# Cross attention, self attention and a ternary feed-forward on one core: 180 waits in a branch not taken, another DVE order in the self stage, gathers and buffers at the stage ends

## The chip, the cores and the metric

One core of one Trainium2 chip runs the whole program. The time is that of the device for one execution, in microseconds (us). The engines are called as in the profile: PE (TensorE), DVE (VectorE), ACT (ScalarE), POOL (GpSimd), SP (SyncE, which here issues the DMAs).

## The reference

x is 64 batches of 64 tokens by 512, the context 64 batches of 512 keys by 512. All is fp32; 16 heads of 32.

```python
x = x + cross_attention(layernorm(x), ctx, ctx, mask)      # mask: True keys get -inf
x = x + self_attention(layernorm(x))   # scores * mask of the 64 largest of 64: a plain softmax
x = x + ffn(layernorm(x))              # relu(x @ Wq1.T + b1) @ Wq2.T + b2, 512 -> 2048 -> 512

def _quantize(W):                      # the two weights of the feed-forward
    gamma = jnp.mean(jnp.abs(W))
    return jnp.clip(jnp.round(W / (gamma + EPS)), -1.0, 1.0)
```

The mask of batch 0 holds for all. It leaves keys of the last of four tiles of 128 alone, so the kernel takes the branch that works on that tile only.

## The kernel before, in words

Products are made in pairs of fp32r values: each operand is split into a high part (a copy to fp32r) and a low part (the rest, by a subtraction on DVE), and `split_products` (L340 to L350) issues three matmuls for each chunk of 128. The feed-forward's weights are -1, 0 or 1, so there only the moving side is split.

There are three stages, each with its own program on each engine, in order: cross attention in 16 units of 256 tokens, self attention in 16 units of 256, feed-forward in 8 units of 512. `run_steps` writes out units 0 and 1, puts two units into the body of a hardware loop, and writes out the last two ("last_but_one", "last"). So the self loop's body is two units and runs six times, with five jumps back; the feed-forward loop's runs twice. `choose` reads a flag and runs the cross program for the last key tile (the If branch) or the one for all tiles (the Else branch), which stands behind it in each engine's instructions; the self and feed-forward programs come after both.

The order of the work is written out by hand, engine by engine, and semaphores carry the dependences. Two PSUM banks `project_0/1` take all projections in turn (class `Banks`); a product waits until its bank's last contents were copied out.

One self unit on PE (`self_pe`, step at L1460): scores of token tile 0, the output product O1 of the unit before (o_proj waits on the low half of the attended values, `self_at_lo`), queries of the next unit Q0, Q1, scores of tile 1, transposes of tile 0's probabilities, keys K0, attention product of tile 0, K1, values V0, transposes 1, V1, attention product 1, O0. On DVE (`self_dve`, step at L1665): maxima(0) (a reduction L1611 and a subtraction L1613), residual of O1 (L1630), statistics of the unit after next, divide(0) (L1619, L415, L419), normalise (L464, which waits for the POOL's reciprocal root L1177), block transpose (L427), maxima(1), the high and low half of the attended values (L1590, L1594), divide(1), keys_out (L546), values_out twice (L552), the low part of the next x (`self_x_lo`, L531), then in the loop two ternary quantisations of feed-forward weights (L1232, L1235), residual of O0, the low half for tile 1. `self_ln_gather` lets SP issue four DMAs (L435) that bring the transposed blocks into place; ACT then makes the high part of x (L527, after V1 is done) and DVE the low part.

At the end of cross attention the units' last steps already prepare the self stage: `self_ln_normalise` and `self_ln_transpose` for self units 0 (S_FIRST) and 1 (S_SECOND), whose gathers SP issues (L631, L641), the second one after the store of cross token tile 0. At the end of the self stage `last_step` on DVE (L1634) prepares feed-forward unit 0 (F_FIRST): `ff_x_norm` is one buffer of two token tiles, so tiles 2 and 3 are normalised after the low part of tiles 0 and 1 is made. In feed-forward the same steps stand between the splits of the hidden values (L1822 to L1829).

## Time and profile before

| | us |
|---|---|
| median of 3 runs | 1780.06 (1777.68 to 1786.38) |
| profiled execution | 1779.26 |
| its span, first to last instruction | 1777.4 |
| granted PE clock, mean | 0.982 |
| PE busy / DVE busy / ACT busy / POOL busy | 1678.3 / 1068.4 / 697.7 / 215.0 |

```profile
PE   6899999999999999969989889899789999999999
PEclk9899999999999999989999999999999999999999
PE 83%; DVE 7%; issue 4%; ACT 3%; DMA 2%; POOL 1%; SPq 0%; DVEq 0%; POOLq 0%; ACTq 0%
q8 instruction: 145, 2.38, 0.6%
```

The first two lines cut the span into 40 slices of 44 us and give the busy share of PE and the clock granted to it in tenths (9 is 90% or more). The third splits the chain of work that ended last by engine; "issue" is time in which nothing that the profile shows was waited for. The fourth is the DMA queue that brings instructions: packets, MB, share of the DMA engines. Cross attention runs to about 790 us, self attention to about 1313, feed-forward to the end.

### The profile page before, as it was taken

To read this page: it belongs to the slowest core of one execution; us is meant where nothing else is said; L and a number is where in the kernel's file an instruction comes from. 1 tells how busy PE (TensorE), PEld (TensorE's weight loads), DVE (VectorE), ACT (ScalarE), POOL (GpSimd) and SP (SyncE) were. 2 spreads that over 40 slices of the span, in tenths; PEclk is the share of its full clock that TensorE was granted. 3 is DMA by queue.
4 is the path that set the end of the run, shared out by engine and by line. 5 is a ranking of instruction groups with operands and counts; after the bars stand their busy time and mean duration, and the time that the engine had idled before them with its cause. 6 is when DMAs were issued, how large, how long until landed. Compare 5 with 4: busy or idle time off the path is not lost.

```text
span 1777.4 us, 38416 instructions
## 1 busy us (share of the span) xinstructions
PE 1678.3 (94%) x16012; PEld 1401.2 (79%) x16012; DVE 1068.4 (60%) x1492; ACT 697.7 (39%) x1657; POOL 215.0 (12%) x300
## 2 busy tenths in 40 slices
PE   6899999999999999969989889899789999999999
PEld 4788888888888888858878778788678888888887
DVE  3655555555555555757767767767766555556543
ACT  2555555555555555647222222222222222222221
POOL 1000000000000000112121121121130222012200
PEclk9899999999999999989999999999999999999999
DMA  6011111111111112433111111211212121112110
GB/s 214 13 60 60 61 61 60 61 60 61 60 61 60 60 53 72 172 116 104 61 38 49 61 38 49 61 38 49 81 58 62 34 71 60 60 24 71 36 36 24
DMA packets 83529, 112.52 MB, mean 63 GB/s; under 512 B 7840, under 2 KB 48928, under 8 KB 82080
## 3 DMA queue, kind: packets, MB, share of 16 engines
q1 hardware_dynamic: 83360, 109.95, 19.6%
q8 instruction: 145, 2.38, 0.6%
q14 instruction: 24, 0.20, 0.0%
HBM read 67.97 MB, written 25.17 MB: 52 GB/s over the span
## 4 chain that ended last, share of the span: by engine, by line
PE 83%; DVE 7%; issue 4%; ACT 3%; DMA 2%; POOL 1%; SPq 0%; DVEq 0%; POOLq 0%; ACTq 0%
PE project L347 45%; PE project L1282 13%; PE scores L715 4%; PE scores L1775 3%; PE scores L1773 3%; PE probs_t_psum L1775 3%; PE probs_t_psum L1773 3%; PE probs_t_psum L724 3%; PE attended_t L741 2%; PE probs_t_psum L1391 1%; PE scores L519 1%; PE attended_t L1410 1%; DMA x<-self_residual 1%; DVE self_residual L1630 1%; DVE self_scores_shifted L1613 1%
## 5 line engine op out<-in xcount | busy, mean ns | idle before, releaser
L1282 PE MATMUL project<-ff_xt,w_ternary 128*128 128x512 f32 x1024 | 253.1, 389 | 0.0
L1282 PEld LDWEIGHTS project<-ff_xt,w_ternary 128*128 128x128 f32 x1024 | 192.2, 188 | 40.1 <-issue 0.2
L1292 ACT ACTIVATE hidden<-project,b_sb 128x512 f32<-128x512 f32 x128 | 88.2, 689 | 339.8 <-PE project L1282 339.8
L901 ACT ACTIVATE cross_scores_probs<-cross_scores_probs,exp_bias,logit_scale 128x128 f32<-128x128 f32 x256 | 122.7, 482 | 101.9 <-DVE exp_bias L1044 101.9
L347 PE MATMUL project<-self_xt_hi,self_w_hi 128*128 128x256 f32 x512 | 149.5, 292 | 7.0 <-DVE self_xt_lo L531 6.0
L347 PE MATMUL project<-self_xt_lo,self_w_hi 128*128 128x256 f32 x512 | 145.9, 285 | 0.0
L347 PE MATMUL project<-self_xt_hi,self_w_lo 128*128 128x256 f32 x512 | 145.7, 285 | 0.0
L901 ACT ACTIVATE cross_probs<-cross_scores,exp_bias,logit_scale 128x128 f32<-128x128 f32 x256 | 122.8, 483 | 1.6 <-DVE exp_bias L1044 1.6
L347 PE MATMUL project<-ctx_hi,cross_w_hi 128*128 128x512 f32 x256 | 106.5, 416 | 15.2 <-DVE ctx_lo L1063 15.2
L347 PE MATMUL project<-cross_w_hi,ctx_hi 128*128 128x512 f32 x256 | 108.7, 425 | 0.0
L347 PEld LDWEIGHTS project<-self_xt_hi,self_w_hi 128*128 128x128 f32 x512 | 99.3, 194 | 10.2 <-issue 6.9
L347 PE MATMUL project<-ctx_hi,cross_w_lo 128*128 128x512 f32 x256 | 101.4, 396 | 0.0
L347 PE MATMUL project<-ctx_lo,cross_w_hi 128*128 128x512 f32 x256 | 101.3, 396 | 0.0
L347 PE MATMUL project<-cross_w_hi,ctx_lo 128*128 128x512 f32 x256 | 100.6, 393 | 0.0
L347 PE MATMUL project<-cross_w_lo,ctx_hi 128*128 128x512 f32 x256 | 100.3, 392 | 0.0
L347 PEld LDWEIGHTS project<-self_xt_lo,self_w_hi 128*128 128x128 f32 x512 | 99.5, 194 | 0.6
L347 PEld LDWEIGHTS project<-self_xt_hi,self_w_lo 128*128 128x128 f32 x512 | 99.2, 194 | 0.0
L480 POOL TENSOR_TENSOR self_residual<-self_x,bo_sb 128x512 f32<-128x512 f32 x32 | 52.8, 1672 | 370.4 <-DMA x<-self_residual 370.4
L918 ACT ACTIVATE cross_probs_t<-probs_t_psum 128x1024 f32<-128x1024 f32 x64 | 65.3, 1021 | 81.2 <-PE probs_t_psum L724 81.2
L1297 DVE CAST hidden_hi_a<-hidden 128x512 fp32r<-128x512 f32 x64 | 29.0, 453 | 109.1 <-ACT hidden L1292 109.1
L1523 ACT ACTIVATE self_probs<-self_scores_shifted 128x1024 f32<-128x1024 f32 x32 | 33.9, 1060 | 152.8 <-DVE self_scores_shifted L1613 152.8
L1186 POOL TENSOR_TENSOR var_eps<-mean_var,ln_eps 128x2 f32<-128x2 f32 x16 | 5.1, 316 | 646.5 <-DVE mean_var L1008 646.5
(169 smaller groups left out, 4085.7 us busy)
## 6 DMA issues: line engine op xcount, KB each, us to landing
ctx_raw<-in_ctx SPq DMA_DIRECT2D x64, 256.0 KB, 3.9
cross_xt_raw<-in_x_t SPq DMA_DIRECT2D x64, 128.0 KB, 2.1
cross_x<-in_x SPq DMA_DIRECT2D x32, 256.0 KB, 2.9
x<-cross_x SPq DMA_DIRECT2D x32, 256.0 KB, 2.0
self_x<-x SPq DMA_DIRECT2D x32, 256.0 KB, 2.8
self_x_norm<-self_blocks_t SPq DMA_DIRECT2D x64, 128.0 KB, 2.9
ff_w_raw<-in_w SPq DMA_DIRECT2D x2, 4096.0 KB, 14.6
x<-self_residual SPq DMA_DIRECT2D x32, 256.0 KB, 2.0
```

The source lines that it names most:

```text
L347: last = nc.tensor.matmul(out_ap, a, b, start=(n == 0), stop=(n == 3 * len(pairs) - 1))
L480: e.tensor_tensor(sres[:, parity(v), t, :], sx[:, parity(v), t, :], bo_sb[:], ALU.add).then_inc(G.res, 1)
L715: last = nc.tensor.matmul(S[half:half + SEQ, slot * n:(slot + 1) * n], cq_t[rows, c, K.batch(q), :], keys, start=True, stop=True)
L724: last = nc.tensor.transpose(PT[:, i * P:i * P + P], c_p[q % 2][:, i * P:i * P + P], ident[:])
L741: last = nc.tensor.matmul(PV[rows, t, col:col + SEQ], cv[:, parity(u), q if K.kt == 1 else k, DK * head:DK * head + DK], c_pt[:, at:at + S ...
L901: last = nc.scalar.activation(c_p[buf][:, cols], c_s[buf][:, cols], ACT.Exp, bias=exp_bias[:, buf, g:g + 1], scale=logit_scale[:, parity(u ...
L918: nc.scalar.activation(c_pt[:], PT[:], ACT.Copy).then_inc(C.pt_ready, 1)
L1282: last = nc.tensor.matmul(PJ[m % 2][:], w1_q[:, c, cols], x_t[parity(v)][:, c].rearrange("p n a r -> p (n a r)"), start=(c == 0 and x_t is ...
L1292: nc.scalar.activation(h_raw[:, m % 2, :], PJ[m % 2][:], ACT.Relu, bias=b1_sb[:, m:m + 1]).then_inc(h_relu, 1)
L1523: nc.scalar.activation(s_p[:], s_d[:], ACT.Exp, scale=SCORE_SCALE) \
L1773: nc.tensor.matmul(YB[t], h_hi[m % 4][:, rows], w2_q[:, m, :], start=(m == 0), stop=False)
L1775: last = nc.tensor.matmul(YB[t], h_lo[m % 4][:, rows], w2_q[:, m, :], start=False, stop=(m == FC - 1))
```

## The change

Five edits. (1) In the Else branch of `choose`, which is not run here, PE gets 180 waits on a semaphore that has long been set. (2) In the self unit, DVE does maxima(1) before normalising, the block transpose after divide(1), and the two quantisations between the values' copies. (3) At the end of cross attention, DVE divides tile 2 and makes the low half of tile 0 before it normalises S_FIRST, and SP issues the gather of S_SECOND before the store of cross tile 0. (4) The feed-forward's normalised x gets a second buffer, `fxn_1`; at the end of the self stage tiles 2 and 3 are normalised one step earlier, and the residual and maxima(1) come before the transpose and the low part. (5) In the feed-forward units, the normalising of tiles 2 and 3 and the second transpose move to earlier places.

```diff
+            fxn_1 = sb(st, "ff_x_norm_1", [P, 2, D])
+            fxn = [fxn_0, fxn_1]
...
                     e.dma_start(w_raw[:, 0].rearrange("p k n -> p (k n)"), w1).then_inc(fw_in[0], 16)
+                    self_ln_gather(e, S_SECOND)
...
                     if kind == "last" and t == K.nt - 1:
 
-                        self_ln_gather(e, S_SECOND)
                         load_self_x(e, Unit(1, 0))
...
                 values_out(u, v, 1)
+                divide(u, 2)
+                if K.nt == 2:
+                    a_lo(u, 0)
                 if not ahead:
                     self_ln_normalise(e, S_FIRST)
                     self_ln_transpose(e, S_FIRST)
-                divide(u, 2)
-                if K.nt == 2:
-                    a_lo(u, 0)
                 values_out(u, v, 2)
...
-            wait(e, fxt_lo_ready, total(v, 2, t // 2))
-            nc.vector.tensor_scalar(fxn[:, t % 2, :], fx[:, parity(v), t, :],
+            wait(e, fxt_lo_ready, total(v, 2, t // 2 - 1))
+            nc.vector.tensor_scalar(fxn[t // 2][:, t % 2, :], fx[:, parity(v), t, :],
...
             def last_step(u):
                 maxima(u, 0)
-                ff_x_lo(e, F_FIRST, 0)
                 values_out(None, u, 0)
                 divide(u, 0)
-                for t in range(2, FT):
-                    ff_ln_normalise(e, F_FIRST, t)
-                ff_ln_transpose(e, F_FIRST, 1)
                 residual(later(u, -1), 1, "last_but_one")
                 maxima(u, 1)
+                ff_ln_transpose(e, F_FIRST, 1)
+                ff_x_lo(e, F_FIRST, 0)
                 values_out(None, u, 1)
...
                 divide(u, 0)
                 if kind == "full":
                     self_ln_aggregate(e)
+                maxima(u, 1)
+                if kind == "full":
                     self_ln_normalise(e, w)
-                    self_ln_transpose(e, w)
-                maxima(u, 1)
                 a_hi(u)
                 a_lo(u, 0)
                 divide(u, 1)
+                if kind == "full":
+                    self_ln_transpose(e, w)
                 keys_out(u, v, kind)
                 if kind == "full":
                     values_out(u, v, 0)
+                    if not isinstance(u.half, int):
+                        for n in range(2):
+
+                            ternary(e, n, number(u) - 2, lambda k: total(u, 2, k - 4))
                     values_out(u, v, 1)
                     self_x_lo(e, w)
-                    if not isinstance(u.half, int):
-                        for n in range(2):
-
-                            ternary(e, n, number(u) - 2, lambda k: total(u, 2, k - 4))
                 else:
...
                     ff_ln_transpose(e, F_FIRST, 0)
+                    for t in range(2, FT):
+                        ff_ln_normalise(e, F_FIRST, t)
...
-                        if m in (2, 3, 6, 7):
-                            ff_ln_normalise(e, v, (0, 1, 2, 3)[(2, 3, 6, 7).index(m)])
-                        if m in (3, 7):
-                            ff_ln_transpose(e, v, m // 4)
+                        if m in (2, 3, 4, 5):
+                            ff_ln_normalise(e, v, m - 2)
+                        if m in (3, 6):
+                            ff_ln_transpose(e, v, m // 3 - 1)
...
+        PE_FILLER = 180
+
+        def choose(e, program, filler=0):
...
                 program(e, ALL_TILES)
                 e.nop()
+                for _ in range(filler):
+                    e.wait_ge(flag_ready, 1)
...
-            choose(e, cross_pe)
+            choose(e, cross_pe, PE_FILLER)
```

## Rows read from the trace of the kernel before

**Rows 1.** Busy time by stage: us, PE, PEld, DVE, ACT, POOL, PEclk, DMA, GB/s.

```profile
850.00:1245.00 395.00, 361.80 (x5046) 317.62 (x5049) 278.78 (x372) 98.78 (x144) 61.43 (x72) 0.97 0.18 50
1313.00:1777.40 464.40, 460.50 (x2032) 381.11 (x2030) 251.81 (x413) 100.19 (x140) 70.45 (x88) 1.00 0.17 49
```

**Rows 2.** The same view, stretches of the self loop.

```profile
860.30:1224.74 364.44, 331.91 (x4577) 291.15 (x4576) 256.62 (x340) 90.55 (x132) 56.02 (x67) 0.96 0.18 50
890.97:928.02 37.05, 31.95 (x418) 27.79 (x417) 23.46 (x31) 8.22 (x12) 5.61 (x8) 0.91 0.17 45
928.02:958.70 30.68, 29.00 (x417) 25.63 (x416) 23.44 (x30) 8.23 (x12) 4.90 (x7) 1.00 0.19 53
```

**Rows 3.** Timeline of PE at a jump back: start, us, operation, [idle before, releaser].

```profile
912.62 0.61 PE L519 MATMUL scores<-self_k_t,self_q_t 32*64 32x64 f32 x25 [1.92 <-issue]
915.95 1.34 PE L519 MATMUL scores<-self_k_t,self_q_t 32*64 32x64 f32 x39 [2.71 <-issue]
```

**Rows 4.** Instruction queues in 912:979 (self), 1420:1537 and 1539:1655 (feed-forward).

```profile
q8 instruction: 9, 0.15, 1.0%
...
q8 instruction: 4, 0.07, 0.2%
...
q14 instruction: 1, 0.01, 0.0%
```

**Rows 5.** Timeline of PE at the start of a unit without a jump.

```profile
946.86 0.39 PE L347 MATMUL project<-self_w_hi,self_at_lo 128*128 128x512 f32 x1
...
950.02 0.47 PE L347 MATMUL project<-self_w_hi,self_at_hi 128*128 128x512 f32 x1 [1.68 <-DVE self_at_lo L1594]
```

**Rows 6.** Timeline of DVE there.

```profile
943.56 0.69 DVE L552 TENSOR_TENSOR self_v<-project,bv_sb 128x512 f32<-128x512 f32 x1 [2.92 <-PE project L347]
...
945.87 0.48 DVE L1232 TENSOR_SCALAR ff_weight_scratch<-ff_w_raw,thresholds 128x512 f32 x1
...
947.93 0.75 DVE L1235 SCALAR_TENSOR_TENSOR w_ternary<-ff_w_raw,thresholds,ff_weight_scratch 128x512 f32 x1
...
949.20 0.68 DVE L1594 TENSOR_TENSOR self_at_lo<-attended_t,self_at_hi 128x512 fp32r<-128x512 f32 x1
```

**Rows 7.** Timelines of DVE and PE at the end of unit 1, without quantisation.

```profile
848.85 0.69 DVE L1594 TENSOR_TENSOR self_at_lo<-attended_t,self_at_hi 128x512 fp32r<-128x512 f32 x1
...
849.69 0.38 PE L1491 MATMUL attended_t<-abs_total,ones 128*128 128x2 f32 x2 [1.51 <-DVE abs_total L1700]
```

**Rows 8.** Timeline of DVE in the middle of a unit.

```profile
962.29 1.25 DVE L427 STREAM_TRANSPOSE self_blocks_t<-self_x_norm 128x1024 f32<-128x1024 f32 x1
...
965.82 0.68 DVE L1590 CAST self_at_hi<-attended_t 128x512 fp32r<-128x512 f32 x1
...
968.67 1.23 DVE L419 TENSOR_TENSOR self_probs<-self_probs,row_scale 128x1024 f32<-128x1024 f32 x1
```

**Rows 9.** End of cross attention: PE timeline, page's DMA issues, chain.

```profile
721.50 0.74 PE L724 MATMUL probs_t_psum<-ident,cross_scores_probs 128*128 128x128 f32 x5 [1.97 <-DVE cross_scores_probs L419]
...
self_x_norm<-self_blocks_t SPq DMA_DIRECT2D x64, 128.0 KB, 2.9
ff_w_raw<-in_w SPq DMA_DIRECT2D x2, 4096.0 KB, 14.6
...
760.79 1.25 DVE self_blocks_t L427
...
773.33 0.62 SPq L435
...
775.35 3.67 DMA self_x_norm<-self_blocks_t
...
781.56 7.49 PE project L347 x36
```

**Rows 10.** End of the self stage: the chain.

```profile
1287.54 4.36 PE project L347 x12
```

**Rows 11.** The chain: 12 matmuls of 512 columns at full clock.

```profile
722.56 2.75 PE project L347 x12
```

More of the change, by code:

```diff
@@ L244, in build @@
             fres = sb(st, "ff_residual", [P, 2, 4, D])
-            fxn = sb(st, "ff_x_norm", [P, 2, D])
+            fxn_0 = sb(st, "ff_x_norm_0", [P, 2, D])
             f_ln_t = sb(st, "ff_blocks_t", [P, 2 * D])
@@ L254, in build @@
             b2_sb = sb(st, "b2_sb", [P, D])
+            sb(st, "ff_gap_2", [P, 8])
+            fxn_1 = sb(st, "ff_x_norm_1", [P, 2, D])
+            fxn = [fxn_0, fxn_1]
             h_hi = [t[:, i, :] for t in (h_hi_a, h_hi_b) for i in range(2)]
@@ L1260, in ff_ln_transpose @@
             wait(e, f_ln_in, total(v, 128, 64 * n))
-            ln_blocks(fxn[:], f_ln_t[:]).then_inc(f_ln_t_done, 1)
+            ln_blocks(fxn[n][:], f_ln_t[:]).then_inc(f_ln_t_done, 1)
         def ff_ln_gather(e, v, n):
             wait(e, f_ln_t_done, total(v, 2, n + 1))
-            ln_gather(e, fxn[:], f_ln_t, f_ln_in)
-        fx_chunks = fxn[:].rearrange("p t (a c r) -> p c (t a) r", a=4, r=32)
+            ln_gather(e, fxn[n][:], f_ln_t, f_ln_in)
+        fx_chunks = [xn[:].rearrange("p t (a c r) -> p c (t a) r", a=4, r=32) for xn in fxn]
         def ff_x_hi(e, v, n):
             wait(e, f_ln_in, total(v, 128, 64 * n + 64))
-            nc.scalar.activation(fxt_hi[parity(v)][:, :, n], fx_chunks, ACT.Copy).then_inc(fxt_hi_ready, 1)
+            nc.scalar.activation(fxt_hi[parity(v)][:, :, n], fx_chunks[n], ACT.Copy).then_inc(fxt_hi_ready, 1)
         def ff_x_lo(e, v, n):
             wait(e, fxt_hi_ready, total(v, 2, n + 1))
-            nc.vector.tensor_tensor(fxt_lo[parity(v)][:, :, n], fx_chunks,
+            nc.vector.tensor_tensor(fxt_lo[parity(v)][:, :, n], fx_chunks[n],
                                     fxt_hi[parity(v)][:, :, n].bitcast(F32), ALU.subtract).then_inc(fxt_lo_ready, 1)
@@ L1680, in step @@
                     values_out(u, v, 0)
-                    values_out(u, v, 1)
-                    self_x_lo(e, w)
                     if not isinstance(u.half, int):
@@ L1686, in step @@
                             ternary(e, n, number(u) - 2, lambda k: total(u, 2, k - 4))
+                    values_out(u, v, 1)
+                    self_x_lo(e, w)
                 else:
@@ L1860, in ff_pool @@
             run_steps(e, F_UNITS, step)
-        def choose(e, program):
+        PE_FILLER = 180
+        def choose(e, program, filler=0):
             e.wait_ge(flag_ready, 1)
```

## The prediction

> **What bounds the kernel now.** I read the page's shares first (TensorE busy 94%, on 83% of the last chain), then the busy time by stage. Feed-forward is full, 460 us of TensorE in 464; the self loop has 362 in 395 [rows 1]. There TensorE waits, and there the change works.
>
> Next, the self loop by half-iteration, from one second scores product to the next. Without the jump back it takes 30.68 us at full clock; with the jump up to 37.05 at 0.91 of it [rows 2]. The 364.44 us of the group's first row hold six plain and five jumping stretches, so the five jumps cost 364.44 - 11 x 30.68 = 27.0 us. The matmul timeline shows how: after the last output product TensorE idles 1.92 us, runs 25 score matmuls, idles 2.71 us, and then works slowly: the other 39 take 1.34 us [rows 3]. "Issue" is the releaser: no semaphore was late. Instruction traffic says what was: in one iteration nine blocks of 16 KB are fetched (0.15 MB) [rows 4].
>
> The body of that loop has, as compiled, 1,692 TensorE instructions: 832 matmuls with a weight load each and 28 others. The 25 matmuls are 50 instructions behind two others at its head, so a block of 256 ends 52 in and the loop begins at place 204 of a block. 204 + 1,692 = 1,896, which touches 8 blocks; the ninth fetch is the one ahead. The feed-forward loop (1,062 instructions, 5 blocks) is fetched in its first pass and not in its second: 4 blocks, then none [rows 4]. So TensorE's store keeps a loop of 5 blocks and one ahead, and loses one of 8 and one ahead; 7 and one ahead lies between. Of the sizes 6, 7 and 8 that this leaves I take 8, the power of two.
>
> The other wait is at every unit's start: TensorE ends the first scores and stands 1.68 us before the output product, released by the low half of the attended values on DVE [rows 5]. That ran at 949.20, behind two weight quantisations that end at 948.68 [rows 6].
>
> **The change, part by part.**
>
> *180 waits in the branch not taken.* They are never run; they move what stands behind. In the compiled program one semaphore instruction carries two such waits, so I count 90 instructions: the loop begins at 204 + 90 - 256 = 38, and 38 + 1,692 = 1,730 touches 7 blocks. 180 single ones would give 128 + 1,692 = 1,820, 8 blocks. For a jump into kept blocks the bounds are 0 (no idle over 0.25 us stands at the feed-forward jump) and today's whole excess. I take 0, the feed-forward's, since 7 and one ahead fit a store of 8: **-27.0 us**. Feed-forward stays at 5 blocks. The cross loop lies before the filler, unchanged.
>
> The Trainium skill has a rule against this part (Runtime: NRT & Kernel Launch, Instruction fetch mechanics): prefetch is sequential over a window of two pages, and a taken branch outside it stalls for a fetch. By it the feed-forward loop's second pass would have fetched; the trace shows that it did not. The same section gives the PE 2,048 instructions, 8 blocks, by which the -27.0 holds.
>
> *Quantisation ahead of the second values.* Two of them take 948.68 - 945.87 = 2.81 us. DVE idles 2.92 us before that copy [rows 6]: they fit, with 0.1 to spare. Then nothing but the residual precedes the low half. The unit without quantisation shows what is left: output product ended 849.69 - 1.51 = 848.18, low half ended 849.54, 1.36 later [rows 7]. From a product end at 947.25 that is 948.61, and TensorE starts 0.14 behind it (950.02 against 949.88) at 948.75 instead of 950.02: 1.27 us a unit. The loop runs 12 units. At five of their ends the wait is covered by the jump today, but my 30.68 included it: 12 x 1.27 = **-15.2 us**, between 0 and 12 x 1.68 = 20.2.
>
> *Second maxima before normalising; block transpose after the second division.* Today normalising waits for POOL's root, the transpose runs from 962.29 for 1.25 us [rows 8], and only then come the maxima. The exponentials come sooner, but TensorE does not wait for them in the loop: 0. The transpose's move is the price. The division still hangs on the attention product before it: cast at 964.6, 4.1 us to the division's end (as 965.82 to 969.90 now [rows 8]), so 968.7; the transpose ends at 969.9 instead of 963.5. The gather's four DMAs behind it on SP take from 4.9 us (three issues of 0.65 and the median landing of 2.9) to 5.69 (773.33 to 779.02, after 11 us of idle queue) [rows 9], landing at 974.8 to 975.6. ACT wants them at 974.5, so the high and low parts of x come up to 1.1 us late, the low part ending at 978.0; the residual behind it on DVE waits for the product that ends at 978.13. Cost 0, with 0.1 us to spare. The key copy behind the transpose keeps its time. SP's store behind the gather waits for that later product anyway.
>
> *End of cross attention.* The division now precedes the self normalisation and transpose, which held it; TensorE waited for it 1.97 us, until 721.50 [rows 9]. **-2.0**. What is pushed back, the third values copy to 722.9, is wanted at 723.8. On SP the second self gather moves ahead of the first store: blocks are ready at 762.04, issued only at 773.33 [rows 9]. The 4 MB weight load before it on the queue goes out some 16 us before and takes 14.6 [rows 9], so it has landed. So it lands near 768 instead of 779.02, and the next bound is ACT's last copy of probabilities, done at 774.85: x parts done 4.25 us sooner, **-4.3**. The 36 matmuls behind took 7.49 us [rows 9]; at full clock 12 of 512 columns take 2.75 [rows 11], and 24 of 256 columns as much, with a little at the seams 5.6. With 1.7 us idle instead of 6.0 I count the drop gone (1.97 drew none above): **-1.9**. The cross store that the gather now precedes waits for a later product (773.33) in any case.
>
> *End of the self stage.* The second normalised buffer lets tokens 2 and 3 be normalised early (+1.0 us before the first maxima), and the residual that frees the bank goes ahead of transpose and low part. Now: low part, values, division, normalising, transpose, residual, product at 1287.54 [rows 10]. After: maxima until 1277.45, exponentials 1278.55, division 1281.35, residual 1282.0, product 1282.05. Low part and transpose then fall between second maxima and second values; the chain to the last output product keeps 11.35 of its 11.51 us: **-5.6**, down to 0 if the low part binds again, up to 7.2 if the slow product (4.36 for 12 [rows 10], 2.75 at full clock [rows 11]) speeds up.
>
> *Feed-forward order and buffer.* TensorE has no idle there [rows 1]; cover is 464 us of its own work: 0.
>
> Sum: 27.0 + 15.2 + 2.0 + 4.3 + 1.9 + 5.6 = 56.0. The profiled execution took 1,779.26 us (span 1,777.4), 0.8 under the median of 1,780.06. 1,779.3 - 56.0 = 1,723.3; on the median 1,724.
>
> **Rivals.**
> *One fetch at each jump, whatever the blocks.* The first block then has 218 instructions, some 6.5 us of work, so the second stall goes and only the 1.6 to 1.9 us one stays: 5 x 1.6, net of the low-half wait it covers, +8: **1,732**. For: the first pass of every loop fetches. Against: feed-forward's second pass. The skill's two-page rule, above, is this case.
>
> *Still 8 blocks* (the filler counts 180, or the store keeps under 8). With 128 instructions in the first block both stalls stay. Left are 7 x 1.27 + 13.8 = 22.7: **1,757**. Against: the two waits to an instruction.
>
> *The order gives little.* 0.1 us to spare at two places; half of it and the self end lost, about 15 us: **1,739**.
>
> *Slower: the late gather.* DVE runs in order, so a gather later than about 975.7 delays x's low part, residual, low half and TensorE one for one, in 14 units. To eat 56 us it must be 4 us later in each, so take over 9.8 us where 4.9 to 5.7 are seen [rows 9]; at 10.5 it costs 14 x 4.7 = 66: **1,790**. The loop's lighter queue speaks against.
>
> **How the numbers follow.** Forecast 0.76 (own range 1,717 to 1,734: the upper bounds of two terms give 5.0 and 1.6 more, the clock's 1.9 and half the order's 7.6 may fail), one fetch 0.10, order 0.05, 8 blocks 0.07, slower 0.02. 1,717 to 1,740 takes in the first three and leaves out 0.09. A measurement of this kernel tells about 0.5% (9 us) from no change. Faster by more than that: the first four cases but for 0.02 in which a late gather eats most, 0.96; the same 0.02; slower 0.02.
>
> **What would show it.** Instruction fetches in a loop pass after the first: 0, not 9. Every half-iteration near 29.4 us at clock 1.00; no issue wait in the scores. The wait on the low half near 0.4 us. The self gather issued near 760 and landed by 768; the product at 1287.54 some 5.5 us sooner relative to the loop's end. Wrong would be: nine fetches still, DVE waiting on the high part of x past the output product, or a new TensorE wait on the values' bank.

## The result and the profile after

The changed kernel takes **1,724.86 us** (median of 4 runs, 1,723.93 to 1,727.79) against 1,778.87 (4 runs, 1,776.09 to 1,786.38) for the one before: a ratio of 0.9693, 95% interval 0.9660 to 0.9725. The forecast was 1,724.0. The profiled execution of after took 1,724.65 us, its span 1,722.8, against 1,779.26 and 1,777.4 before. Line numbers are now 3 higher than those of before in most places, up to 5 at the end of the file (matmuls of the projections at L350, scores L522, low half L1597).

The page of after, its busy shares, the granted clock, the chain by engine and the instruction queue:

```profile
PE 1662.9 (97%) x16012; PEld 1390.8 (81%) x16012; DVE 1068.9 (62%) x1492; ACT 699.8 (41%) x1657; POOL 212.0 (12%) x300
PEclk9999999999999999999999999999899999999999
PE 91%; DVE 5%; issue 1%; ACT 1%; DMA 1%; SPq 0%; DVEq 0%; ACTq 0%
q8 instruction: 100, 1.64, 0.4%
```

TensorE went from 94% to 97% of the span, its share of the last chain from 83% to 91%, "issue" from 4% to 1%. The instruction queue brings 100 blocks where it brought 145: the five jumps back of the self loop fetched nine each.

Busy time by stretch in after (columns as in [rows 1]): eleven half-iterations of the self loop between the same products as in [rows 2], one of them, self unit 0, and the feed-forward stage:

```profile
854.77:1177.06 322.29, 317.26 (x4578) 281.26 (x4577) 256.31 (x341) 92.00 (x132) 53.74 (x68) 1.00 0.19 54
884.10:913.36 29.26, 28.84 (x418) 25.55 (x417) 24.42 (x32) 8.36 (x12) 3.96 (x7) 1.00 0.19 55
785.11:811.79 26.68, 21.08 (x293) 18.00 (x293) 19.20 (x22) 20.22 (x44) 6.07 (x5) 0.94 0.48 179
1260.00:1722.80 462.80, 458.85 (x2025) 379.74 (x2023) 250.63 (x412) 100.22 (x140) 69.65 (x88) 1.00 0.17 49
```

364.44 us of loop became 322.29, the clock 0.96 became 1.00, and 317.26 us in it are TensorE's work. The DMA view of after from 896 to 1,190 us, which holds all five jumps, has no row for the instruction queue q8 at all; at a jump and at a unit's start the matmul timeline shows:

```profile
932.41 0.39 PE L350 MATMUL project<-self_w_hi,self_at_lo 128*128 128x512 f32 x1
932.73 1.16 PE L522 MATMUL scores<-self_k_t,self_q_t 32*64 32x64 f32 x64
934.30 0.47 PE L350 MATMUL project<-self_w_hi,self_at_hi 128*128 128x512 f32 x1 [0.41 <-DVE self_at_lo L1597]
```

The 64 matmuls of the scores are one group without an idle time where [rows 3] has 1.92 and 2.71 us, and the wait on the low half is 0.41 us where [rows 5] has 1.68. DVE there, the rows that answer to [rows 6]:

```profile
926.13 0.48 DVE L1235 TENSOR_SCALAR ff_weight_scratch<-ff_w_raw,thresholds 128x512 f32 x1
...
928.18 0.75 DVE L1238 SCALAR_TENSOR_TENSOR w_ternary<-ff_w_raw,thresholds,ff_weight_scratch 128x512 f32 x1
929.06 0.69 DVE L555 TENSOR_TENSOR self_v<-project,bv_sb 128x512 f32<-128x512 f32 x1
930.78 1.23 DVE L534 TENSOR_TENSOR self_xt_lo<-self_x_norm,self_xt_hi 128x1024 fp32r<-128x1024 f32 x1 [1.03 <-ACT self_xt_hi L530]
932.83 0.69 DVE L1633 TENSOR_TENSOR self_residual<-project,self_residual 128x512 f32<-128x512 f32 x1 [0.83 <-PE project L350]
933.46 0.69 DVE L1597 TENSOR_TENSOR self_at_lo<-attended_t,self_at_hi 128x512 fp32r<-128x512 f32 x1
```

The quantisations now end before the second values' copy, and DVE stands idle 0.83 us ahead of the residual: it is on time. x itself comes later than before: ScalarE's high part (929.69) now waits for the gather, 0.67 us behind the end of the V1 product (929.02) where it was 0.12 in before. In the first unit of the loop the gather is later still, and there it does cost something: ScalarE waits 3.77 us for the DMA, and TensorE 0.88 us for the low half instead of 0.41.

Where the 54.6 us of span went, from the starts of the same matmuls in both traces. A half-iteration is one unit of the self loop, and the loop's markers are the second scores products of units 2, 13 and 14:

| stretch | forecast | measured |
|---|---|---|
| start of the program, nothing changed there | 0 | -2.95 |
| cross division ahead of normalising (its gap 1.97 to none) | -2.0 | -2.14 |
| second gather (idle time 6.00 to 1.64) | -4.3 | -4.31 |
| clock behind it (36 matmuls 7.48 to 7.35) | -1.9 | -0.1 |
| self unit 0 (23.41 to 26.68) | 0 | +3.3 |
| self unit 1, to unit 2's second scores (42.31 to 42.98) | 0 | +0.7 |
| eleven half-iterations (27.0 + 11 x 1.27) | -41.0 | -42.15 |
| one more, the loop's last | -1.27 | -1.7 |
| end of the self stage, to the last output product | -5.6 | -5.3 |
| feed-forward, its first product to the last matmul's end (468.2 in both) | 0 | 0.0 |

The first row is no effect: the matmul that ends at 764.53 in before and 759.44 in after ended between 759.5 and 764.2 in the ten experiments whose code is that of after up to there, so the trace of after is the luckiest of eleven. That most of the spread between runs of one kernel lies in that stretch is likely, but not shown: one trace of each kernel was kept.

### The profile page after: what moved, and what is told of

It is laid out like the page before. It is cut to its first block, busy times and chain, and to the rows that moved or that the text cites. A ratio compares the mean times of both kernels' runs of the same rounds, so it can differ in the third digit from the quotient of the medians.

```text
span 1722.8 us, 38414 instructions
## 1 busy us (share of the span) xinstructions
PE 1662.9 (97%) x16012; PEld 1390.8 (81%) x16012; DVE 1068.9 (62%) x1492; ACT 699.8 (41%) x1657; POOL 212.0 (12%) x300
## 3 DMA queue, kind: packets, MB, share of 16 engines
q8 instruction: 100, 1.64, 0.4%
## 4 chain that ended last, share of the span: by engine, by line
PE 91%; DVE 5%; issue 1%; ACT 1%; DMA 1%; SPq 0%; DVEq 0%; ACTq 0%
PE project L350 51%; PE project L1285 13%; PE scores L718 4%; PE scores L1780 3%; PE scores L1778 3%; PE probs_t_psum L1780 3%; PE probs_t_psum L1778 3%; PE probs_t_psum L727 3%; PE attended_t L744 2%; PE probs_t_psum L1394 2%; PE attended_t L1413 1%; PE scores L522 1%; DVE self_at_lo L1597 1%; DVE self_residual L1633 1%; DVE row_sum L1622 0%
## 5 line engine op out<-in xcount | busy, mean ns | idle before, releaser
L1285 PEld LDWEIGHTS project<-ff_xt,w_ternary 128*128 128x128 f32 x1024 | 192.1, 188 | 39.8
L350 PE MATMUL project<-self_xt_hi,self_w_hi 128*128 128x256 f32 x512 | 149.2, 291 | 2.7 <-DVE self_xt_lo L534 1.6
L350 PE MATMUL project<-self_xt_lo,self_w_hi 128*128 128x256 f32 x512 | 145.8, 285 | 0.0
L350 PE MATMUL project<-self_xt_hi,self_w_lo 128*128 128x256 f32 x512 | 145.7, 285 | 0.0
L350 PE MATMUL project<-ctx_hi,cross_w_hi 128*128 128x512 f32 x256 | 106.1, 414 | 14.8 <-DVE ctx_lo L1066 14.8
L350 PE MATMUL project<-cross_w_hi,ctx_hi 128*128 128x512 f32 x256 | 108.7, 425 | 0.0
L350 PEld LDWEIGHTS project<-self_xt_hi,self_w_hi 128*128 128x128 f32 x512 | 99.2, 194 | 5.7 <-issue 2.6
L350 PE MATMUL project<-ctx_hi,cross_w_lo 128*128 128x512 f32 x256 | 101.3, 396 | 0.0
L350 PE MATMUL project<-ctx_lo,cross_w_hi 128*128 128x512 f32 x256 | 101.1, 395 | 0.0
L350 PE MATMUL project<-cross_w_hi,ctx_lo 128*128 128x512 f32 x256 | 100.7, 393 | 0.0
L350 PE MATMUL project<-cross_w_lo,ctx_hi 128*128 128x512 f32 x256 | 100.3, 392 | 0.0
L350 PEld LDWEIGHTS project<-self_xt_lo,self_w_hi 128*128 128x128 f32 x512 | 99.3, 194 | 0.6
L350 PEld LDWEIGHTS project<-self_xt_hi,self_w_lo 128*128 128x128 f32 x512 | 99.1, 194 | 0.0
L1300 DVE CAST hidden_hi_a<-hidden 128x512 fp32r<-128x512 f32 x64 | 29.4, 460 | 105.0 <-ACT hidden L1295 105.0
L1300 DVE CAST hidden_hi_b<-hidden 128x512 fp32r<-128x512 f32 x64 | 28.8, 449 | 88.1 <-ACT hidden L1295 87.2
```

The lines of the kernel that those rows point to most:

```text
L350: last = nc.tensor.matmul(out_ap, a, b, start=(n == 0), stop=(n == 3 * len(pairs) - 1))
L1285: last = nc.tensor.matmul(PJ[m % 2][:], w1_q[:, c, cols], x_t[parity(v)][:, c].rearrange("p n a r -> p (n a r)"), start=(c == 0 and x_t is ...
L1300: nc.vector.tensor_copy(h_hi[m % 4], h_raw[:, m % 2, :]).then_inc(h_hi_ready, 1)
```

## Experiments

All times are medians of 4 runs (5 where the text says so); "before" is the kernel before on the same chip in the same job, 1,777.5 to 1,781.4 us in the four jobs. Differences to after join two jobs, and before's own median moved by 3.9 us from job to job: totals that differ by less than some 4 us decide nothing, and there the trace has to.

**The filler alone, on the kernel before.**

```diff
+        PE_FILLER = 180
-        def choose(e, program):
+        def choose(e, program, filler=0):
...
+                for _ in range(filler):
+                    e.wait_ge(flag_ready, 1)
...
-            choose(e, cross_pe)
+            choose(e, cross_pe, PE_FILLER)
```

> The kernel before with the 180 waits alone; nothing else is changed. Theory (the fetches): the loop begins at place 38 and touches 7 blocks, so no instruction block is fetched in any pass after the first; the five jumping half-iterations (364.44 - 6 x 30.68 = 180.36 us, 36.07 each) become plain ones of 30.68, with the 1.68 us wait on the low half now at every unit's start: -27.0 us against before, about 1,752. Rival (the filler matters little, the loop's gain came from the order of DVE's work): 0 to -5, nine fetches in each pass as before.

Measured 1,753.39 us against 1,777.49: -24.1, ratio 0.9877 (0.9853 to 0.9901). Eleven half-iterations and one of them:

```profile
859.08:1197.82 338.74, 319.77 (x4578) 282.04 (x4577) 256.97 (x341) 90.68 (x132) 56.11 (x68) 1.00 0.18 51
921.50:952.21 30.71, 29.06 (x417) 25.63 (x416) 23.35 (x31) 8.24 (x12) 5.15 (x7) 1.00 0.17 51
```

25.7 us of the loop are gone (364.44 to 338.74), all half-iterations but the first two (31.4 and 31.0) take the 30.7 us that [rows 2] has for one without a jump, and the queue q8 brings no instruction block between 905 and 1,190 us. The wait on the low half stands at every later unit's start (1.64 us). The rival is out: instructions that never run gave 24 us.

**The kernel after without the filler.**

```diff
-        PE_FILLER = 180
+        PE_FILLER = 0
```

> The kernel after with no waits put in: the loop begins at place 204 and touches 8 blocks. Theory: nine fetches in each later pass; the six plain half-iterations stay at 29.26 us and the five jumping ones are as long as before, 36.07 each, since the order of DVE's work saves nothing where the fetch stall covers the low half: +5 x 6.8 = +34 us against after, about 1,759. Rival 1 (the two savings simply add, as the sum of the prediction treated them from before's side): +27, 1,752. Rival 2 (with the new order the stall hides behind other work): under +15.

Measured 1,757.43 us, 32.6 above after. All eleven half-iterations, and one of the five that jump:

```profile
857.76:1210.22 352.46, 327.19 (x4577) 289.23 (x4576) 257.95 (x341) 91.84 (x132) 53.85 (x67) 0.96 0.18 51
886.96:922.00 35.04, 30.60 (x418) 26.90 (x417) 23.36 (x32) 8.35 (x12) 5.03 (x7) 0.95 0.17 47
```

Both stalls are back (1.73 and 2.71 us at the first jump, 25 scores matmuls between them), and nine blocks are fetched in each pass. The loop takes 30.2 us more; a jumping half-iteration is 35.0 to 35.7, near the 36.07 of before, though DVE's order is the new one. By the first rival it would be 34.7 (29.26 + 27 / 5), so the theory is the nearer, if not exact; the second rival is out. So the two changes don't simply add up: in the loop the filler alone gave 25.7 us, the new order alone 12.0 (364.44 to 352.46), both together 42.1, since the new order without the filler leaves the jumping stretches nearly as they were. An issue wait of 1.07 us also comes back in straight code, in the first scores of the last self unit. It costs nothing: the V1 product behind it waits 2.28 us instead of 3.33 and starts 26.17 us behind unit 14's second scores, as in after.

**296 and 320 waits: which end of the 8-block limit?** The same one line as above, with 296 and with 320.

> The kernel after with 296 waits instead of 180. If two waits make one instruction (148), the loop begins at place 96 and ends at 96 + 1,692 = 1,788, still 7 blocks of 256: no fetches in later passes, the time of after within 3 us. If each wait were an instruction, it would begin at place 244, touch 8 blocks and lose 25 to 34 us. If the limit were on the loop's length in another way (a place within a block that matters), something between.

> The kernel after with 320 waits: 160 instructions, loop from place 108 to 1,800, which is 8 blocks by 8 instructions. Theory (a store of 8 blocks that holds 7 and the one ahead): nine fetches in every later pass. The first block now has 148 of the loop's instructions, so the first product of scores and ten more matmuls are ready before the second block is needed: the first stall (1.9 us, net of the 0.4 us wait it covers) stays, the second goes, and the clock may drop for a while: 5 x 1.5 to 5 x 4 = +7 to +20 us against after, and more than the kernel with 296 waits by the same. Rival (the store holds 8 blocks and what fails is something else about place 204): no fetches, the time of after.

With 296, 1,724.21 us: the time of after, no fetch after the first pass. With 320, 1,730.73: +5.9 on after, +6.5 on the kernel with 296. In the compiled program the loop stands 148 and 160 instructions further on than without waits. That agrees with the runs: with one instruction to a wait the kernel with 296 would have touched 8 blocks. And 12 instructions more are what brings the fetches back. But not all of them. The kernel with 320 runs its second pass (905 to 958 us) and its last two (1,073 to 1,195) without a row for the instruction queue; between 960 and 1,020 it has

```profile
q8 instruction: 9, 0.15, 1.3%
```

and its matmul timeline at the first jump and at the second:

```profile
903.75 1.16 PE L522 MATMUL scores<-self_k_t,self_q_t 32*64 32x64 f32 x64
905.32 0.47 PE L350 MATMUL project<-self_w_hi,self_at_hi 128*128 128x512 f32 x1 [0.41 <-DVE self_at_lo L1597]
...
964.58 1.16 PE L522 MATMUL scores<-self_k_t,self_q_t 32*64 32x64 f32 x64 [2.37 <-issue]
...
968.47 0.39 PE L350 MATMUL project<-self_w_lo,self_at_hi 128*128 128x512 f32 x1 [0.92 <-issue]
```

So a loop of 8 blocks was kept over three jumps of five and lost over two, with no fall of the clock behind the lost ones. Their half-iterations took 32.3 and 30.9 us, 4.9 us together over the 29.2 of the others. My expectation of nine fetches in every pass was wrong, and so was the rival's of none. At both lost jumps two blocks are fetched within 0.8 us of each other (960.4 and 960.5, 1,021.4 and 1,022.2); at the kept ones none is. The reading: the store holds 8 blocks; the ninth, the one ahead, displaces the loop's first, and with only 8 instructions left behind the last boundary the jump at times comes before the ninth is asked for.

**404 waits: 50 instructions into the eighth block.**

> The kernel after with 404 waits: 202 instructions, loop from place 150 to 1,842, 8 blocks and 50 instructions into the last of them. With 160 instructions, 8 into the last block, three of the five jumps fetched nothing and two fetched nine blocks and cost some 2.45 us each. Theory (the store holds the loop's 8 blocks; what loses them is the one ahead, and with 8 instructions left it was asked for ahead of the jump only at times): with 50 instructions left it is asked for ahead of every jump, so all five fetch nine blocks, with one stall each: 5 x 2.45 = +12 us against after, about 1,737. Rival (8 blocks are kept or lost by chance, whatever the place): again one to three jumps without fetches, 1,728 to 1,733.

Measured 1,754.38 us, +29.5. All five jumps fetch, two blocks within 0.8 us at each of them, nine blocks a pass (this one 960 to 1,024 us):

```profile
q8 instruction: 9, 0.15, 1.1%
```

That bears the reading out: what loses the loop is the block ahead. The price I expected was too low: with 106 instructions before the first boundary both stalls are there (the scores split 51 and 13, where 52 pairs fill 104 of the 106 places), and the clock falls behind them:

```profile
905.45 1.57 PE L522 MATMUL scores<-self_k_t,self_q_t 32*64 32x64 f32 x51 [1.87 <-issue]
908.72 0.69 PE L522 MATMUL scores<-self_k_t,self_q_t 32*64 32x64 f32 x13 [1.70 <-issue]
909.34 0.80 PE L350 MATMUL project<-self_w_hi,self_at_hi 128*128 128x512 f32 x1
909.94 0.63 PE L350 MATMUL project<-self_w_lo,self_at_hi 128*128 128x512 f32 x1
```

The last row's 0.63 us is 0.40 at full clock (row 932.41 of after has 0.39). A jump costs about 5.9 us here (29.5 / 5), clock included, and about 2.5 (4.9 / 2) where 148 instructions stand before the boundary and the clock stays up.

**The quantisation back behind x's low part.**

```diff
                     values_out(u, v, 0)
-                    if not isinstance(u.half, int):
-                        for n in range(2):
-                            ternary(e, n, number(u) - 2, lambda k: total(u, 2, k - 4))
                     values_out(u, v, 1)
                     self_x_lo(e, w)
+                    if not isinstance(u.half, int):
+                        for n in range(2):
+                            ternary(e, n, number(u) - 2, lambda k: total(u, 2, k - 4))
```

> The kernel after with the two weight quantisations put back behind the values' second copy and x's low part; nothing else. Theory (they stood between the output product and its low half): TensorE waits 1.68 us again at each unit's start in the loop, 1.27 more than the 0.41 of after, in 12 units: +15.2 us, about 1,739 to 1,740. Rival (the second maxima and the later transpose brought the low half forward, not the quantisation): within 3 us of after.

Measured 1,754.03 us: +29.2, twice the expectation. DVE's timeline, and a half-iteration at full clock:

```profile
1003.58 1.23 DVE L534 TENSOR_TENSOR self_xt_lo<-self_x_norm,self_xt_hi 128x1024 fp32r<-128x1024 f32 x1 [1.00 <-ACT self_xt_hi L530]
1004.72 0.48 DVE L1235 TENSOR_SCALAR ff_weight_scratch<-ff_w_raw,thresholds 128x512 f32 x1
...
1008.05 0.68 DVE L1597 TENSOR_TENSOR self_at_lo<-attended_t,self_at_hi 128x512 fp32r<-128x512 f32 x1
```

```profile
1017.52:1048.52 31.00, 28.77 (x418) 25.58 (x417) 23.12 (x31) 8.35 (x12) 4.88 (x7) 1.00 0.17 51
```

TensorE waits 2.2 to 2.3 us for the low half, not 1.68: in the new order the transpose comes later, x with it, and the quantisations behind it end later too. That is 31.00 - 29.19 = 1.8 us a half-iteration (29.19 with 296 waits, same code); the rest, 350.37 - 11 x 31.00 = 9.4 us over the eleven half-iterations, lies in four: the first, where x's gather is late and TensorE idles 4.25 us at the unit's start, and three in which the clock fell behind some 2.2 us of idle time (13.5 to 13.7 us from unit start to second scores in place of 12.0 to 12.1). The rival is out.

**Normalise and transpose back ahead of the second maxima.**

```diff
-                maxima(u, 1)
                 if kind == "full":
                     self_ln_normalise(e, w)
+                    self_ln_transpose(e, w)
+                maxima(u, 1)
                 a_hi(u)
                 a_lo(u, 0)
                 divide(u, 1)
-                if kind == "full":
-                    self_ln_transpose(e, w)
```

> The kernel after with normalising and transposing put back ahead of the second maxima in the self units (quantisation stays ahead). Theory: in the loop TensorE did not wait for the second exponentials, so a half-iteration stays at 29.26 us; in unit 0 the second exponentials come later, so GpSimd's 128x2048 low part of the output weights no longer lies ahead of DVE's second division, and the 2.01 and 0.75 us of idle TensorE at 801.24 and 804.31 of after go: -3 us against after, 1,721 to 1,723. Rival (the move is what shortened the loop): half-iterations over 29.5 and +5 us or more.

Measured 1,726.51 us, +1.6: no difference that these runs can tell. The trace decides, and shows both halves: unit 0 is 23.8 us long again and its two gaps are gone, and the half-iterations from the third on are 29.34 to 29.47, 0.2 longer. With the two kernels above and that with 296 waits this makes a square of half-iterations at full clock:

| | quantisation behind | quantisation ahead |
|---|---|---|
| old order | 30.71 | 29.4 |
| new order | 31.00 | 29.19 |

The new order is worth 0.2 us when the quantisation is ahead, and costs 0.3 when it is not.

**The cross stage: gather back, division back** (two kernels).

```diff
-                    self_ln_gather(e, S_SECOND)
                 for t in range(K.nt):
...
                     if kind == "last" and t == K.nt - 1:
+                        self_ln_gather(e, S_SECOND)
```

```diff
+                if not ahead:
+                    self_ln_normalise(e, S_FIRST)
+                    self_ln_transpose(e, S_FIRST)
                 divide(u, 2)
                 if K.nt == 2:
                     a_lo(u, 0)
-                if not ahead:
-                    self_ln_normalise(e, S_FIRST)
-                    self_ln_transpose(e, S_FIRST)
```

> The kernel after with the second self gather put back behind the first cross store. Theory: TensorE's idle before the last Q0 product of the cross stage goes from 1.64 back to 6.0 us, +4.3 us and no more, since the clock fell behind the short idle time too (36 matmuls in 7.35 us against 7.48 before): 1,729. Rival (something else of the order opened that wait): under +1.

> The kernel after with the division of the last but one cross unit put back behind the self stage's first normalising and transpose. Theory: TensorE's 1.97 us of idle before the transposes (719.53 of before) come back: +2.0 us, about 1,727, which lies near what the runs tell apart, so the gap in the matmul timeline decides. Rival (the first gather, then on its way 1.2 us sooner, gives part of it back later): the gap is there, and the total rises by less than 1 us.

Measured 1,730.06 (+5.2) and 1,726.89 us (+2.0, less than two jobs can tell, so the gap must carry it). The matmul timelines of the two, in this order:

```profile
778.27 0.55 PE L350 MATMUL project<-self_xt_hi,self_w_hi 128*128 128x256 f32 x1 [5.92 <-DVE self_xt_lo L534]
```

```profile
721.11 1.06 PE L727 MATMUL probs_t_psum<-ident,cross_scores_probs 128*128 128x128 f32 x8 [1.96 <-DVE cross_scores_probs L422]
```

5.92 us against 1.64 in after, and 1.96 against none: both terms as forecast. In the second kernel the whole 2 us are still there at the next wait of TensorE (55.83 us from the probabilities' transposes at 710.57 to those at 766.40, 53.71 in after), so nothing was given back.

**The self stage's end back**, on the two buffers.

```diff
                 maxima(u, 0)
+                ff_x_lo(e, F_FIRST, 0)
                 values_out(None, u, 0)
                 divide(u, 0)
+                for t in range(2, FT):
+                    ff_ln_normalise(e, F_FIRST, t)
+                ff_ln_transpose(e, F_FIRST, 1)
                 residual(later(u, -1), 1, "last_but_one")
                 maxima(u, 1)
-                ff_ln_transpose(e, F_FIRST, 1)
-                ff_x_lo(e, F_FIRST, 0)
...
                     ff_ln_transpose(e, F_FIRST, 0)
-                    for t in range(2, FT):
-                        ff_ln_normalise(e, F_FIRST, t)
```

> The kernel after with the last self unit's DVE order of before (low part of x ahead of the values, tokens 2 and 3 normalised and transposed behind the first division, then the residual), on the two buffers. Theory: TensorE's idle before the last V1 product goes from 3.33 back to about 7.7 us or a little more, and the last output products come 5.3 us later relative to unit 14: +5.3 us, about 1,730. Rival (the two buffers alone bring the gain, by letting tokens 2 and 3 be normalised early): under +2.

Measured 1,731.08 us, +6.2. The V1 product in this kernel, and in after:

```profile
1240.54 0.79 PE L350 MATMUL project<-self_w_hi,self_xt_hi 128*128 128x512 f32 x1 [9.01 <-DVE self_residual L1633]
```

```profile
1232.46 0.50 PE L350 MATMUL project<-self_w_hi,self_xt_hi 128*128 128x512 f32 x1 [3.33 <-DVE self_residual L1633]
```

TensorE waits 9.01 us for the residual instead of 3.33, and the V1 product starts 31.58 us behind unit 14's second scores against 26.16: +5.4. The order brings the gain; the two buffers by themselves bring none.

**Two stalls mended, not in either kernel** (5 rounds). The trace of after has unit 0 longer by 3.3 us than before, with two waits of TensorE that before has not:

```profile
803.24 1.07 PE L1394 MATMUL probs_t_psum<-ident,self_probs 128*128 128x128 f32 x8 [2.01 <-DVE self_probs L422]
805.06 0.50 PE L350 MATMUL project<-self_w_hi,self_xt_hi 128*128 128x512 f32 x1 [0.75 <-DVE self_k_t L549]
```

DVE there:

```profile
798.04 0.26 DVE L418 RECIPROCAL row_scale<-row_sum 128x16 f32<-128x16 f32 x1
798.33 4.77 DVE L422 TENSOR_TENSOR self_probs<-self_probs,row_scale 128x1024 f32<-128x1024 f32 x1
803.02 1.23 DVE L430 STREAM_TRANSPOSE self_blocks_t<-self_x_norm 128x1024 f32<-128x1024 f32 x1
```

and GpSimd:

```profile
797.40 4.61 POOL L410 TENSOR_TENSOR self_w_lo<-self_w_raw,self_w_hi 128x2048 fp32r<-128x2048 f32 x1 [6.57 <-ACT self_w_hi L404]
```

A multiply that takes 1.23 us where GpSimd stands idle takes 4.77, and ends 1.09 us behind the end of GpSimd's operation, which began first. In before the order of the two is the other way round:

```profile
807.83 1.22 DVE L419 TENSOR_TENSOR self_probs<-self_probs,row_scale 128x1024 f32<-128x1024 f32 x1
```

```profile
808.48 5.05 POOL L407 TENSOR_TENSOR self_w_lo<-self_w_raw,self_w_hi 128x2048 fp32r<-128x2048 f32 x1 [7.92 <-ACT self_w_hi L401]
```

The multiply keeps its time, and it is GpSimd's operation that is longer, 5.05 us for 4.6. A smaller case stands in the loop of both kernels: GpSimd's additions of the output bias begin just ahead of the first division's multiply, which in before then takes 2.17 us:

```profile
956.32 3.50 POOL L480 TENSOR_TENSOR self_residual<-self_x,bo_sb 128x512 f32<-128x512 f32 x2 [25.62 <-DMA x<-self_residual]
```

```profile
956.52 2.17 DVE L419 TENSOR_TENSOR self_probs<-self_probs,row_scale 128x1024 f32<-128x1024 f32 x1
```

TensorE does not wait for that one. The edits, the second in short:

```diff
-                if is_unit(u, 0):
-                    self_w_hi(e, 3)
                 magnitudes(u, 6, 9)
+                if is_unit(u, 0):
+                    self_w_hi(e, 3)
...
+            def weight_sums():
+                e.wait_ge(fw_abs, 1)
+                nc.tensor.matmul(W_SUMS, ones[:], abs_total[:], start=True, stop=True) \
+                    .then_inc(fw_total, 1)
...
-                    o_proj(u, 0, kind)
+                    o_proj(u, 0, kind, weight_sums if is_unit(u, 1) else None)
...
                     values_out(u, v, 1)
+                    if is_unit(u, 1):
+                        e.wait_ge(fw_summed, 2 * FC)
+                        nc.vector.reduce_sum(abs_total[:], abs_sum[:], AXIS.X).then_inc(fw_abs, 1)
                     self_x_lo(e, w)
```

The matmul now stands half way through the output product, the two thresholds follow x's low part, and ScalarE's high half of unit 1 waits for the first threshold.

> The kernel after with two edits that are in neither kernel. In unit 0 ScalarE makes the high part of the output weights three magnitudes later, so that GpSimd's low part (128x2048, 4.6 us) starts behind DVE's second division instead of across it. And in unit 1 the sum of magnitudes, its matmul and the two thresholds are done beside the output product instead of behind it. Theory (GpSimd's operation holds up DVE's multiply of two SBUF operands until it has ended): the multiply takes 1.23 us instead of 4.77, the idle of 2.01 and 0.75 us in unit 0 goes, and the 1.51 and 0.44 us at 841.11 become about 0.4 for the last low half, with the clock no longer falling there (1.5 us): -2.7 and -3, in all 1,718 to 1,720. Rival (the multiply was long for another reason): it stays over 3 us and unit 0 keeps its length of 26.7 us.

Measured 1,717.02 us, ratio to before 0.9641 (0.9626 to 0.9655), 7.8 below after. DVE and GpSimd in unit 0:

```profile
800.55 1.23 DVE L422 TENSOR_TENSOR self_probs<-self_probs,row_scale 128x1024 f32<-128x1024 f32 x1
801.69 1.24 DVE L430 STREAM_TRANSPOSE self_blocks_t<-self_x_norm 128x1024 f32<-128x1024 f32 x1
```

```profile
801.74 4.62 POOL L410 TENSOR_TENSOR self_w_lo<-self_w_raw,self_w_hi 128x2048 fp32r<-128x2048 f32 x1 [9.38 <-ACT self_w_hi L404]
```

The multiply takes 1.23 us, unit 0 24.1, and unit 1 to the second scores of unit 2 39.8 instead of 43.0. That is 5.7 us by the trace, as forecast, and the rival is out. The medians give 2 more, which no experiment here assigns. The profiled run does not settle it: at 1,720.65 us it is the slowest of the five, 4.8 us later than after's by 764.23, and from there to unit 0's second scores it is 3.2 us quicker, with the clock staying up at the end of the cross stage.

**The end of the self stage, further** (5 rounds), on top of that.

```diff
                 values_out(None, u, 0)
-                divide(u, 0)
                 residual(later(u, -1), 1, "last_but_one")
+                divide(u, 0)
...
                 values_out(None, u, 1)
-                divide(u, 1)
                 a_hi(u)
                 a_lo(u, 0)
+                divide(u, 1)
                 ff_x_lo(e, F_FIRST, 1)
```

> The kernel of the two stalls mended (1,717.0) with two more moves in DVE's last self unit: the residual that frees the bank goes ahead of the first division, into the 0.5 us in which DVE waits for the exponentials, and the attended values' high and low part go ahead of the second division. Theory: the V1 product waits for the residual alone, so it starts some 3 us sooner and the idle of 3.33 us shrinks to 0.5; and the output product's 4.23 us of idle, which were a division and two copies, become about 1.5 us: -3 and -2.7 less what the transposes then wait, in all -4 to -6 us, 1,711 to 1,713. Rival (the first transposes wait for the division anyway and the chain of exponentials sets the end): -1 or less.

Measured **1,711.49 us** (1,710.35 to 1,714.5), ratio to before 0.9628 (0.9613 to 0.9642); 13.4 below after and 5.5 below the kernel that it builds on, within the forecast of 4 to 6. The V1 product no longer waits, and the output product starts 32.2 us behind unit 14's second scores against 37.9. Its own idle time shrank less than forecast: of 4.23 us 3.42 are left, not 1.5.

## Why the prediction was right, and where its terms were off

The total came out within 1 us of the forecast. The two large terms were right in mechanism, and the experiments show them; two smaller ones failed, and luck helped the sum.

**The five jumps, -27.0.** Right in mechanism and place; alone the filler took 25.7 us off the loop and 24.1 off the median. Undone from after it is worth 30.2 us of loop, since the stall also covers what the new order saves. The count of two waits to an instruction and the limit of 7 blocks and one ahead are shown by the kernels with 296, 320 and 404 waits. The step "of the sizes 6, 7 and 8 I take 8, the power of two" was a guess when written; the passes of 8 blocks without a fetch now show it. What it missed is that 8 blocks need not be lost. The rival of one fetch at each jump is out, and with it, for this loop, the two-page window of the Trainium skill (Runtime: NRT & Kernel Launch, Instruction fetch mechanics): by it every jump back would fetch, and after shows none. The 2,048 instructions that the same section gives the PE agree with the passes of 8 blocks.

**The quantisation, -15.2.** The loop gained 338.74 - 322.29 = 16.5 us over the filler alone, against 11 x 1.27 = 14.0. The rest is the second maxima and the transpose, which I had at 0: 0.2 us a half-iteration. The wait came out at 0.41 us where 0.4 was forecast. The slack that I counted, 0.1 us, was larger: DVE is idle 0.83 us ahead of the residual, because, in part, x came some 0.55 us later than before and not up to 1.1. Only in the loop's first unit was the gather late enough to cost TensorE anything (0.88 us of wait for 0.41), the mechanism of the rival that would have made the kernel slower.

**Cross stage, -2.0 and -4.3.** Both right to 0.1 us, by the traces of the kernels that undo them (1.96 and 5.92 - 1.64 = 4.28).

**The clock behind the gather, -1.9.** Wrong: -0.1. The step that failed is "with 1.7 us idle instead of 6.0 I count the drop gone". The 36 matmuls took 7.35 us behind 1.64 us of idle time, and the granted clock was at its lower level, 1.2 GHz instead of 2.4, from 772.3 to 775.7 (one of 256 columns took 0.41 us there and 0.28 behind it). In nine of the ten experiments with that gap it was so, too; in the kernel with the two stalls mended the same group took 5.86 us behind the same 1.64 us. So the clock's fall there is not settled by the length of that one gap, and what decides it is open.

**Maxima and exponentials earlier, 0.** Right in the loop to 0.2 us, wrong in unit 0: "TensorE does not wait for them in the loop: 0" leaves unit 0 out and took no account of GpSimd. There ScalarE made the weights' high part sooner, GpSimd's 4.6 us operation moved across the division, and 2.01 and 0.75 us of idle TensorE appeared. Undoing the order and moving ScalarE's copy both take it away. The Trainium skill states the mechanism (SBUF — State Buffer, SBUF: two separate sides): DVE and GpSimd share a pair of ports, held by whichever starts first for its whole operation; a DVE operation with two SBUF inputs takes part when GpSimd's reads SBUF. The rows agree: 1.09 us from the end of GpSimd's operation to the multiply's end, and where the multiply began first it kept its 1.22 us and GpSimd's operation took 5.05.

**Unit 1 to 2.** The stretch from unit 2's first scores to its second took 11.34 us against 9.78, with the clock low from 844.0 to 847.4 behind the same 1.51 and 0.44 us of idle time that before has there at full clock [rows 7]. The kernel before with the filler alone has 11.16 us there, so it is not the order's doing; with the idle time mended it was 10.3. Why the clock stayed up behind that idle time in before is open.

**End of the self stage, -5.6.** Right: -5.3, and +5.4 when undone.

**Feed-forward order and buffer, 0.** Right: TensorE takes 468.2 us there in both. No kernel undoes that part alone.

By the trace 5.8 us of the forecast are missing (clock 1.8, unit 0 3.3, unit 1 0.7), and 1.6 us more of loop and the 2.95 us of luck at the start stand against them, which is why the total is closer than its parts.

## What to carry to other kernels

A loop that touches one block of 256 instructions too many can pay on every pass (30 us of 1,757 here), and a few instructions that never run, put ahead of it, can bring it under the limit: count the blocks from the compiled program, leave room for the one that is fetched ahead, and count again after each edit before it. When work moves earlier on one engine, look at what its consumers on the others now overlap: here ScalarE's copy let GpSimd's operation across DVE's critical multiply. And a term measured by undoing one part is worth its value only beside the rest as it stands: the quantisation was worth 1.3 us a half-iteration in the old order and 1.8 in the new.

## What the runs showed of the hardware that I had not expected

- TensorE ran a loop of 8 blocks without a fetch over three jumps of five. Where the block behind the loop was fetched ahead of the jump, all were fetched again, nine in a pass. The jump then cost 2.5 us with 148 instructions ahead of the first block boundary and the clock at full, 5.9 us with 106 and a fall of the clock.
- A DVE multiply with two SBUF operands was held from 1.23 to 4.77 us by a GpSimd operation of 4.61 us that had begun 0.93 us before it; begun 0.65 us before GpSimd's, it kept its 1.22 us, and GpSimd's took 5.05. The block transpose, one SBUF operand, kept its 1.24 us beside the same operation, and GpSimd's its 4.62; there the transpose began 0.05 us first.
- Idle times of 2.2 to 2.3 us at eleven units' starts, with the quantisation back, left the granted clock at 1.00 in most half-iterations; a fall came with three of the eleven. 1.64 us at the end of the cross stage was followed by one in ten traces of eleven. The length of one gap does not tell it.
